# A window-attention kernel: another order of work in the first image, four taps projected by TensorE in the last strips, one reciprocal for both windows

## The reference, cut to what matters

```python
atn = softmax(einsum('nhqc,nhkc->nhqk', qw, kw) * SCALE)
yw = einsum('nhqk,nhkc->nhqc', atn, vw)
local = depthwise3x3(vs, depth_w) + depth_b
y = concatenate([y, v2]); s = (y + local).mean(axis=(2, 3))
ca = sigmoid(conv1x1(leaky_relu(conv1x1(s, fu1_w), 0.2), fu2_w))
y = conv1x1(y * ca + local * (1 - ca), proj_w, proj_b) + x0
```

## Time and profile before

| | |
|---|---|
| median of 3 runs | 1735.08 us (1733.53 to 1736.01) |
| the profiled execution | 1739.07 us, its span 1737.2 us |
| busy in the span | PE 91%, VectorE 79%, ScalarE 47%, GpSimd 13% |
| chain that ended last | PE 59%, VectorE 27%, issue 10%, DMA 2% |

### The profile page before, as it was taken

The page is one execution under the profiler, slowest core; times in us unless marked ns, Lnnn a source line. Parts: engine busy times, 40 slices in busy tenths (PEclk is TensorE's granted clock), DMA queues, the critical chain, the costliest instruction groups (busy, mean ns, idle before and its releaser), DMA issues.

```text
span 1737.2 us, 34686 instructions
## 1 busy us (share of the span) xinstructions
PE 1574.5 (91%) x10491; PEld 958.0 (55%) x10491; DVE 1381.1 (79%) x2570; ACT 816.1 (47%) x1851; POOL 225.7 (13%) x675
## 2 busy tenths in 40 slices
PE   5888898888999999999999999999999999777775
PEld 3666566656666666655666666655666666322221
DVE  3333433345899999998999999989999999899998
ACT  2444444444455555554555555545555555311121
POOL 1111111010111111110111111121111111000000
PEclk9677867787999999999999999999999999978877
DMA  2121211123556655554655665545565556557663
GB/s 54 42 47 38 51 41 36 42 50 75 113 117 123 120 120 118 117 119 96 124 119 118 123 123 122 118 94 110 121 123 123 123 118 119 116 116 140 121 135 84
DMA packets 360938, 174.10 MB, mean 100 GB/s; under 512 B 267760, under 2 KB 333064, under 8 KB 360904
## 3 DMA queue, kind: packets, MB, share of 16 engines
q1 hardware_dynamic: 360904, 173.69, 49.0%
HBM read 108.85 MB, written 63.70 MB: 99 GB/s over the span
## 4 chain that ended last, share of the span: by engine, by line
PE 59%; DVE 27%; issue 10%; DMA 2%; DVEq 1%; SPq 0%; ACT 0%; ACTq 0%
DVE mixed L1067 11%; PE banks_g L572 8%; PE banks_t L523 8%; PE banks_g L579 6%; PE banks_s L487 6%; PE banks_g L462 6%; PE banks_t L495 5%; PE banks_g L470 4%; PE banks_a L523 4%; PE banks_g L574 4%; DVE mx L866 3%; DVE xn L858 3%; DVE zs L1089 3%; DVE bn L837 2%; DMA qd<-nmx 2%
## 5 line engine op out<-in xcount | busy, mean ns | idle before, releaser
L1067 DVE SCALAR_TENSOR_TENSOR mixed<-vin,c_pack,mixed 96x1024 f32<-96x1024 f32 x384 | 494.5, 1288 | 7.5
L572 PE MATMUL banks_g<-vin,proj_t 96*96 96x512 f32 x512 | 268.0, 648 | 30.2 <-DVE zs L1089 26.9
L1078 DVE SCALAR_TENSOR_TENSOR oo<-zs,l_w,oo 96x1024 f32<-96x1024 f32 x192 | 245.4, 1278 | 5.4 <-ACT oo L763 1.3
L713 ACT ACTIVATE vd<-banks_a 64x192 f32<-64x192 f32 x260 | 86.9, 334 | 326.7 <-PE banks_a L476 321.8
L837 DVE BATCH_NORM_STATS2 bn<-banks_a 128x6 f32<-128x96 f32 x528 | 98.8, 247 | 155.4 <-PE banks_a L437 154.9
L727 ACT ACTIVATE pt<-banks_t 128x512 f32<-128x512 f32 x256 | 138.9, 594 | 136.9 <-PE banks_t L495 136.4
L866 DVE TENSOR_REDUCE mx<-banks_s 128x8 f32<-128x512 f32 x260 | 166.9, 683 | 36.0 <-PE banks_s L487 31.5
L487 PE MATMUL banks_s<-km,qd 64*128 64x128 f32 x2080 | 157.1, 292 | 38.6 <-DVE mx L866 36.5
L495 PE MATMUL banks_t<-qd,km 64*128 64x128 f32 x2048 | 169.5, 312 | 16.0 <-DMA qd<-nmx 16.0
L487 PEld LDWEIGHTS banks_s<-km,qd 64*128 64x128 f32 x2080 | 131.2, 194 | 93.4 <-DVE mx L866 79.2
L753 ACT ACTIVATE mixed<-vin,c_pack 96x1024 f32<-96x1024 f32 x64 | 73.5, 1149 | 223.6 <-DMA vin<-v_img 223.6
(11 more groups left out here) (126 smaller groups left out, 1847.1 us busy)
## 6 DMA issues: line engine op xcount, KB each, us to landing
vin<-v_img SPq DMA_DIRECT2D x64, 480.0 KB, 5.6
v_img<-vrow SPq DMA_DIRECT2D x130, 192.0 KB, 2.2
xc<-in_x SPq DMA_DIRECT2D x134, 186.0 KB, 5.6
x<-in_x SPq DMA_DIRECT2D x64, 384.0 KB, 7.3
out<-oo SPq DMA_DIRECT2D x64, 384.0 KB, 3.0
y_img<-ybuf SPq DMA_DIRECT2D x256, 48.0 KB, 1.7
ycat<-v_img SPq DMA_DIRECT2D x64, 192.0 KB, 5.4
ycat<-y_img SPq DMA_DIRECT2D x64, 186.0 KB, 5.5
```

The lines of the kernel that those rows point to most:

```text
L572: mm(banks_g[:C, c, :], proj_t[:, n, :], vin[:, par, at:at + 4, 1 + dw:1 + dw + W], start=n == 0, stop=False)
L1067: v.scalar_tensor_tensor(out=mb[:, par, :, :], in0=vin[:, par, 1 + dh:1 + dh + WS, 1 + dw:1 + dw + W], scalar=depth_w[:, DVE_TAPS[m]:DVE_T ...
L1078: v.scalar_tensor_tensor(out=oo[:, par, :, :], in0=zs[:, at:at + WS, 1 + dw:1 + dw + W], scalar=l1_w[:, n:n + 1], in1=oo[:, par, :, :], op ...
```

## The change

Four edits.

1. The first 16 strips have functions of their own, `alone`, on PE, ScalarE and VectorE. PE begins a strip with `vs_of`, `y_transposed` and `x_transposed`, then the first `scores_transposed`, `keys_queries`, the second `x_transposed`, the second `scores_transposed`, the first `scores`, `rstd_rows`, and the first `values`. Before, it began with `x_transposed` and the first `scores_transposed`. ScalarE begins with `vs_out` and `y_out`, and VectorE does the first `maxima` before `normalise` and `divide`.
2. In these strips the keys leave PSUM by two VectorE `tensor_scalar` in place of two ScalarE activations.
3. `PE_TAPS` has four taps in place of two. The two new ones (6 and 8) are projected by PE only in the last 16 strips (`tail`), where VectorE does four `mix` in place of six; elsewhere VectorE still does them.
4. `divide` takes one reciprocal over 128 rows in place of two over 64.

```diff
-PE_TAPS = (0, 2)
+PE_TAPS = (0, 2, 6, 8)
+JOINED = 2
+DVE_TAPS = tuple(k for k in range(9) if k != ACT_TAP and k not in PE_TAPS) + PE_TAPS[JOINED:]
@@ tensor @@
-                for n, tap in enumerate(PE_TAPS):
+                for n, tap in enumerate(PE_TAPS if last else PE_TAPS[:JOINED]):
...
+            def alone(h, k, y=True):
+                t = 2 * h + k
+                vs_of(t + 1)
+                if y:
+                    y_transposed(t - 1)
+                x_transposed(t + 2, 0)
+                pe.wait_ge(mx_moved, 16 * (t + 1))
+                pe.wait_ge(yq_done, FREE + 4 * t)
+                scores_transposed(k, 0)
+                keys_queries(t + 1)
+                x_transposed(t + 2, 1)
+                pe.wait_ge(pt_done, 4 * t + 2)
+                scores_transposed(k, 1)
+                pe.wait_ge(km_done, 2 * (t + 2))
+                pe.wait_ge(qd_done, 2 * (t + 2))
+                pe.wait_ge(nmx_done, t + 1)
+                scores(1 - k, 0)
+                rstd_rows(t + 2, 0)
+                rstd_rows(t + 2, 1)
+                values(t, k, 0, not y)
+                pe.wait_ge(mx_done, 4 * (t + 1) + 2)
+                scores(1 - k, 1)
+                values(t, k, 1, not y)
+                pe.wait_ge(yq_done, FREE + 4 * t + 2)
+                max_transposed(t + 1)
+                v_transposed()
@@ scalar @@
+            def alone(h, k, y=True):
+                t = 2 * h + k
+                vs_out(t + 1, 0)
+                vs_out(t + 1, 1)
+                if y:
+                    y_out(t - 1, 1 - k, h - 1 + k)
+                exps(t, 0)
+                queries(t + 1, 1 - k)
+                rsqrt(t + 2)
+                exps(t, 1)
+                sum_x(t + 2, 0)
+                sum_x(t + 2, 1)
+                values(t + 1, 1 - k)
@@ vector @@
+                v.reciprocal(rec[:, half, :].rearrange("q (n h) -> q n h", h=2), o[:, :, 0, :, HD]).then_inc(rec_done, 1)
+                dve.wait_ge(rec_done, 2 * t + half + 1)
                 for wi in range(2):
-                    r = slice(wi * K, (wi + 1) * K)
-                    rc = rec[r, half, :].rearrange("q (n h) -> q n h", h=2)
-                    v.reciprocal(rc, o[r, :, wi, :, HD]).then_inc(rec_done, 1)
-                for wi in range(2):
-                    dve.wait_ge(rec_done, 4 * t + 2 * half + wi + 1)
...
+            def keys(s, k):
+                dve.wait_ge(kq_done, 2 * s + 1)
+                for h in range(2):
+                    v.tensor_scalar(km[:, k, :, h, :], banks_g[:, 0, :].rearrange("c (p k) -> c p k", k=K),
+                                    k_scale[:, h:h + 1], k_bias[:, h:h + 1], ALU.mult, ALU.add).then_inc(km_done, 1)
+            def alone(h, k):
+                t = 2 * h + k
+                statistics(t + 2, 0)
+                keys(t + 1, 1 - k)
+                statistics(t + 2, 1)
+                variance(t + 2)
+                maxima(t + 1, 0)
+                normalise(t + 2, 0)
+                normalise(t + 2, 1)
+                divide(t, 0)
+                maxima(t + 1, 1)
+                maxima_out(t + 1)
+                divide(t, 1)
...
                 if cur:
-                    mix(u, par, 3)
-                    mix(u, par, 4)
+                    mix(u, par, 3, tail)
+                if cur and not tail:
+                    mix(u, par, 4, tail)
...
-            strip(h0, 1, attend=False, cur=True, prev=True, gated=B - 1)
+            strip(h0, 1, attend=False, cur=True, prev=True, gated=B - 1, tail=True)
```

More of the change, by code:

```diff
@@ L62, with mixes @@
 NM = len(DVE_TAPS)
+NT = NM - (len(PE_TAPS) - JOINED)
+LAST = (B - 1) * NS
+def mixes(u, last):
+    return NM * u if not last else NM * LAST + NT * (u - LAST)
 L1_TAPS = TAPS[:4]
@@ L574, in project, with project_mixed @@
                 mm(banks_g[:C, c, :], proj_c[:], ycat[:, par, 4 * c:4 * c + 4, :], start=False, stop=False)
-            def project_mixed(u, par):
-                pe.wait_ge(m_step, NM * (u + 1))
+            def project_mixed(u, par, last):
+                pe.wait_ge(m_step, mixes(u + 1, last))
                 for c in range(2):
@@ L580, in project_mixed, with strip @@
                 last.then_inc(z_done, 1)
-            def strip(h, k, attend=True, y=True, cur=False, prev=False, gate=None, gated=None):
+            def alone(h, k, y=True):
[24 more added lines that the diff above has]
+                v_transposed()
+            def strip(h, k, attend=True, y=True, cur=False, prev=False, gate=None, gated=None, tail=False):
                 t = 2 * h + k
@@ L616, in strip @@
                 if cur:
-                    project(u, um, par, 0)
+                    project(u, um, par, 0, tail)
                 if attend:
@@ L628, in strip @@
                 if cur:
-                    project(u, um, par, 1)
+                    project(u, um, par, 1, tail)
                 if gate is not None:
@@ L639, in strip @@
                 if cur:
-                    project_mixed(u, par)
+                    project_mixed(u, par, tail)
                 if gate is not None:
                     one_column(gate, fu2T[:], tr[:, 1:2], 2, C, 3)
-            strip(0, 0, y=False)
-            strip(0, 1)
+            alone(0, 0, y=False)
+            alone(0, 1)
             with pe.Fori(1, NS // 2) as h:
-                strip(h, 0)
-                strip(h, 1)
+                alone(h, 0)
+                alone(h, 1)
             strip(NS // 2, 0, gate=0)
@@ L1059, in filters, with mix @@
                 assert (mid[0], asked[0]) == (N_MID, MID_STEPS), (mid, asked)
-            def mix(u, par, m):
+            def mix(u, par, m, last):
                 if m == 0:
@@ L1064, in mix @@
                 else:
-                    dve.wait_ge(m_step, NM * u + m)
+                    dve.wait_ge(m_step, mixes(u, last) + m)
                 dh, dw = TAPS[DVE_TAPS[m]]
@@ L1090, in finish, with strip @@
                                        in1=x0[:, par, :, :], op0=ALU.add, op1=ALU.add).then_inc(zs_done, 1)
-            def strip(h, k, attend=True, cur=False, prev=False, gate=None, gated=None):
+            def keys(s, k):
[16 more added lines that the diff above has]
+                divide(t, 1)
+            def strip(h, k, attend=True, cur=False, prev=False, gate=None, gated=None, tail=False):
                 t = 2 * h + k
@@ L1103, in strip @@
                 if cur:
-                    mix(u, par, 0)
+                    mix(u, par, 0, tail)
                 if gated is not None:
@@ L1107, in strip @@
                 if cur:
-                    mix(u, par, 1)
+                    mix(u, par, 1, tail)
                 if gated is not None:
@@ L1111, in strip @@
                 if cur:
-                    mix(u, par, 2)
+                    mix(u, par, 2, tail)
                 if gate is not None:
@@ L1132, in strip @@
                     maxima(t + 1, 1)
-                if cur:
-                    mix(u, par, 5)
+                if cur and not tail:
+                    mix(u, par, 5, tail)
                 if attend:
@@ L1150, in strip @@
                     filters(gated, prev)
-            strip(0, 0)
-            strip(0, 1)
+            alone(0, 0)
+            alone(0, 1)
             with dve.Fori(1, NS // 2) as h:
-                strip(h, 0)
-                strip(h, 1)
+                alone(h, 0)
+                alone(h, 1)
             strip(NS // 2, 0, gate=0)
```

15 lines of the change are left out of this document (7 added, 8 removed).

## The result

The changed kernel took 1656.83 us (median of 4 runs, 1647.0 to 1659.62) against 1735.55 for the kernel before on the same chip: ratio 0.953, 95% interval 0.9484 to 0.9576. Measured again beside its variants on another chip it was 0.948 (0.9432 to 0.953). The profiled execution took 1647.0 us, its span 1645.2.

What follows compares the result with a forecast made beforehand. Bounds: PE's waits and low clock in the first stage, PE in the middle, VectorE in the last. From 1739.07 us, -91 - 3 + 1 + 10 = -83 gives 1656; median 4 lower, 1652; range 1620 to 1700.

Steps and rivals of the forecast that it cites:

- The forecast's own sum: Whole kernel: -91 - 3 + 1 + 10 = -83 us against the profiled execution's 1739.07 us, so 1656 us.
- What the new order leaves on PE: First stage: both old PE waits go, one wait of 1.0 us for the second exps stays, 16.1 us a strip.
- one strip in six would fall in clock: First stage: a falling strip loses up to 5.7 us, 0.9 on average, so 17.0 us a strip, 272 in all.
- The rival in which transposes do not hold the clock: First stage: the 1.0 us wait still costs the clock, 20.1 us a strip, gain 42 not 91, total 1701; chance 0.20.
- The reading of the old waits: First stage before: each strip has PE waits of 1.4 us for the maxima's DMA and 1.96 us for VectorE's maxima.
- The keys' price: First stage, VectorE: two tensor_scalar at 0.65 us each, 1.3 together, costing nothing but with no slack behind them.
- The slower rival: First stage: a keys pair of 2.0 us or more makes PE wait 1.7, nothing won there, total 1749; chance 0.04.
- The last stage: Last 15 strips: PE becomes the bound through banks_g, 13.5 us a strip, 203 us against 192, 10 us slower.
- both bounds (12.25 and 13.95): Last stage, us a strip: no strip falls in clock, 9 us faster; all fall, 17 us slower.
- The strips around the last gate: Strip with gated about even; two new proj_t products cost some 0.4 us in each image, 1 us slower.
- The reciprocal: Edit to divide: 0.23 us less VectorE work per divide, nobody waiting for it in the first and last stages.
- The middle stage: 47 strips paced by PE, 98% busy: 3 us gained from the single reciprocal, between 0 and 5.

## Why the prediction was right, point by point

The time (1652 forecast, 1656.8 measured) and its direction were right, and the mechanisms of the two stages that move the time were the ones named. The closeness is partly luck. The forecast's own sum was for the profiled execution, 1656 us, and that took 1647: the first stage came out 16 us better, the last 5 worse, the middle 3 worse, and the strips around the gates 1 better. The step from there to the median was then wrong the other way: the forecast took 4 us off, and the median lies 10 us above the profiled execution, as much as the clock of the first gate's strips makes between two traces, which the sum had nowhere.

- **What the new order leaves on PE.** Forecast: both old waits gone, one new wait of 1.0 us at `rstd_rows` for the second `exps`, a strip of 15.1 + 1.0 = 16.1 us. Measured: 17.0 us in 16 waits of 1.0 to 1.3, a strip of 16.0. The step right behind it, that one strip in six would fall in clock (17.0 us a strip), failed: the clock fell after none of the 16 waits. That term was 256 us in place of 272. A wait of 1.06 us is short enough here, with eight transposes and light matmuls behind it. The rival in which transposes do not hold the clock, which the Trainium skill's page "TensorE: Matmul & The Clock Gate" (Part 4) suggested, did not come; the rows show only that they do no harm behind a wait of this length.
- **The reading of the old waits.** The prediction gave every strip a wait of 1.4 us for the DMA. Eleven of the 16 had only 0.5 to 0.8 us: PE at the low clock uses up part of that wait with slow work. This changes nothing in the forecast for the new order, where the wait goes, but it is why the waits and the clock can't be priced apart by adding up waits.
- **The keys' price.** Forecast 0.65 us each, measured 0.81 (1.53 us for the pair), a fifth over the nearest row. The wait grew by less than that: in the strip shown the second `statistics` start 0.2 us late for it, and ScalarE's `rsqrt` took 0.45 us where 0.53 had been counted. That there is no slack behind the keys was right: 1.4 us more on VectorE cost 1.4 us of waiting a strip and 85 us in all.
- **The slower rival.** It put the whole first stage's gain at risk from a pair of 2.0 us and a wait of 1.7. The run with the keys doubled went further, to four operations in 3.0 us and 2.5 us of waiting, and had 341 us where the rival had 363. Its mechanism is real, but the clock does not fall all the way, so its price was over 20 us too high.
- **The last stage.** Forecast: PE becomes the bound through the hand-over at `banks_g`, 12.25 us a strip at the high clock, 13.5 with three strips in four falling. Measured 12.1 with the wait filled, and 13.84 as it is: thirteen of fifteen strips took 13.78 us or more, and two of them 15.65. The mechanism and both bounds (12.25 and 13.95) held; how often the clock falls was put too low, and two strips lie over the upper bound, with a longer stretch at the low clock. The limit of about 3 us for idle gaps that the Trainium skill's page "TensorE: Matmul & The Clock Gate" gives ("Why this matters for your kernels") does not hold for this kernel: gaps of 1.5 to 1.7 us cost the clock in nearly every strip.
- **The strips around the last gate.** Forecast: 1 us more for edit 3. Measured 3.2 more in the first pair of traces. Over all traces they take 35.9 to 38.6 us with two projected taps and 39.1 to 43.3 with four, so the term was too small by 2 us or more.
- **The reciprocal.** Forecast 3 us in the middle stage, nothing in the others. In the changed kernel no run shows anything of it. The sentence that nobody waits for it in the first stage was false for the old order, where the stage is 26 us shorter with it: I looked for `divide`'s readers and not at what stands behind it on VectorE, the maxima that PE waits for. The new order takes that away, which is why the sum did not suffer.
- **The middle stage.** -3 forecast, -0.1 in the first pair of traces. Its 47 strips take 1046.9 to 1052.1 us in the nine traces with one reciprocal (mean 1049.8) and 1050.3 to 1054.5 in the five with two (mean 1052.0). A gain of some 2 us fits these means, but it is less than the traces of either kind scatter, and they are from several chips.

## What to carry to other kernels

Price a wait of TensorE twice: once as idle time and once as the slower work behind it; here between three fifths and three quarters of a large gain was clock, and spare matmuls in the wait are a cheap experiment that tells the two apart. When work is moved from one engine to another, walk the chain through the buffer that they share before counting the busy time that goes: with one set of banks two engines take turns, and 2.5 us less on VectorE made the strip 1 us longer, while a second set made it 2.5 us shorter. And an operation that nobody reads in time may still stand ahead of one that somebody does.

## What the runs showed of the hardware

Short waits of PE can cost the clock, and small differences between them matter. With one wait of 1.0 to 1.3 us in each strip of 16 us the clock stayed at 2.4 GHz after all 16 of them. With 0.66 and 1.83 us in a strip the clock's mean was 0.80. With 1.5 to 1.7 us between dense 512-column matmuls thirteen strips of fifteen had a stretch at 1.2 GHz, most of them losing 1.7 us. And 0.29 us off a wait of 1.96 moved the mean clock of a stage from 0.76 to 0.84, with PE idle as long in sum as before. The length of the wait is not all of it: in the kernel before, hand-overs of 1.5 to 1.9 us in the last stage were followed by a fall in 5 of the 10 that PE came to at the high clock. These cases differ in the work around the waits too, and no run varied the length alone. Filling the waits with matmuls that nobody reads brought the clock to 1.00 in both stages.
